# Graph softmax: the maxima of all four heads of a row block in one VectorE instruction, with one signal to ScalarE

## The reference, cut to what matters

```python
msg = xl[src] + xr[dst]
act = jnp.where(msg > 0, msg, NEG_SLOPE * msg)
e = jnp.einsum('ehd,hd->eh', act, att)                  # one score per edge and head
m = jax.ops.segment_max(e, dst, num_segments=n)         # maxima per target node and head
p = jnp.exp(e - m[dst])
denom = jax.ops.segment_sum(p, dst, num_segments=n)
alpha = p / (denom[dst] + 1e-16)
out = jax.ops.segment_sum(alpha[..., None] * xl[src], dst, num_segments=n)
return out.reshape(n, HID) @ W_up
...
x = x + _L1_gnn_ref(...) + _L1_mix_ref(...)             # both added to the residual
```

## Time and profile before

| | |
|---|---|
| time, median of 3 runs | 1725.18 us (1722.89 to 1726.66) |
| the profiled execution's own time | 1725.1 us |
| its span | 1722.8 us |
| TensorE busy | 1674.9 us, 97% |
| VectorE busy | 832.2 us, 48% |
| ScalarE busy | 414.4 us, 24% |
| mean granted TensorE clock | 0.992 |

### The profile page before, as it was taken

One profiled execution on the slowest core, in us unless ns is written; L12 is line 12 of the kernel. 1 busy time (PEld: TensorE's weight loads), 2 busy tenths in 40 slices (PEclk: granted clock), 3 DMA queues, 4 the chain that ended last, 5 costly groups with the idle time before them and its releaser, 6 DMA issues. The chain is left out here.

```text
span 1722.8 us, 21026 instructions
## 1 busy us (share of the span) xinstructions
PE 1674.9 (97%) x7904; PEld 1044.3 (61%) x7904; DVE 832.2 (48%) x1642; ACT 414.4 (24%) x771; POOL 654.2 (38%) x537
## 2 busy tenths in 40 slices
PE   8999999998999999999999999998999999999998
PEld 5466445544444677755477776555766766777633
DVE  5888334562722432154455554767654223222237
ACT  1000000001411001111167773662112222222232
POOL 0566886220000047677787873000031322222213
PEclk9999999999999999999999999999999999999999
DMA  9655114553360044333322221634076999999951
GB/s 346 217 140 158 1 2 126 132 173 82 145 233 5 0 116 115 98 98 101 90 52 55 53 58 43 174 114 161 1 197 200 391 414 407 413 412 412 402 142 60
DMA packets 103755, 281.70 MB, mean 164 GB/s; under 512 B 61745, under 2 KB 69155, under 8 KB 91282
## 3 DMA queue, kind: packets, MB, share of 16 engines
q1 hardware_dynamic: 28755, 218.54, 34.5%
q0 software_dynamic: 67872, 50.79, 13.3%
q10 hardware_dynamic: 7052, 11.35, 2.2%
HBM read 250.37 MB, written 29.80 MB: 163 GB/s over the span
## 5 line engine op out<-in xcount | busy, mean ns | idle before, releaser
L1015 POOL DMA_INDIRECT table_d<-wring x85 | 174.6, 2055 | 111.2 <-issue 68.8
L1409 POOL DMA_INDIRECT wring<-xl_d,wring x85 | 108.5, 1276 | 253.8 <-DMA xr_d<-flat_b 227.9
L1422 POOL DMA_INDIRECT score_d<-wring x85 | 110.9, 1305 | 73.0 <-DMA score_d<-wring 46.4
L469 PE MATMUL bank<-flat_d,wring 128*128 128x312 f32 (+1 forms) x512 | 135.0, 426 | 0.0
L3011 PEld LDWEIGHTS bank<-picked_flat,wring 128*128 128x128 f32 x1152 | 129.4, 192 | 7.7 <-issue 7.7
L3011 PE MATMUL bank<-picked_flat,wring 128*128 128x128 f32 x1152 | 131.3, 276 | 0.0
L1409 POOL DMA_INDIRECT wring<-xr_d,wring x85 | 111.3, 1309 | 25.9 <-issue 23.8
L469 PEld LDWEIGHTS bank<-flat_d,wring 128*128 128x128 f32 x512 | 96.9, 189 | 37.7
L3018 PE MATMUL bank<-wring,picked_flat 128*64 128x256 f32 x640 | 73.3, 382 | 1.2 <-PEq L2485 1.2
L1696 PE MATMUL bank<-wring,flat_d 128*125 128x512 f32 x160 | 71.5, 599 | 0.8 <-ACT flat_c L2224 0.5
L3124 PE MATMUL bank<-wring,region_a 128*125 128x512 f32 x160 | 68.9, 593 | 2.7 <-issue 2.7
(11 more groups left out here) (487 smaller groups left out, 2979.5 us busy)
## 6 DMA issues: line engine op xcount, KB each, us to landing
wring<-in_experts SPq DMA_DIRECT2D x57, 2048.0 KB, 19.5
wring<-in_L_Ws SPq DMA_DIRECT2D x6, 2048.0 KB, 16.6
table_d<-eq_buf SPq DMA_DIRECT2D x2, 3072.0 KB, 27.9
score_d<-no_edge SPq DMA_DIRECT2D x2, 3072.0 KB, 32.8
wring<-table_d POOLq DMA_DIRECT2D x10, 610.4 KB, 7.3
wring<-score_d SPq DMA_DIRECT2D x5, 1093.8 KB
wring<-pid_d ACTq DMA_DIRECT2D x17, 312.5 KB
wring<-in_edge_w ACTq DMA_DIRECT2D x17, 312.5 KB
```

The lines of the kernel that those rows point to most:

```text
L469: ins = pe.matmul(bank[:, 0:n], w[:, k * HALF + m * P:k * HALF + (m + 1) * P], act_t[:, k, at:at + n], start=(k == 0), stop=(k == chunks - 1))
L1015: pool.indirect_dma_start(out=tables_d[b % 2], out_offset=bass.IndirectOffsetOnAxis(ap=edge_at[:, b:b + 1], axis=0), in_=edge_sums[:, b, : ...
L1409: pool.indirect_dma_start(out=to[:, g % 2, j, :], out_offset=None, in_=table, in_offset=bass.IndirectOffsetOnAxis(ap=index[:, b:b + 1], ax ...
L1422: pool.indirect_dma_start(out=score_d, out_offset=bass.IndirectOffsetOnAxis(ap=cell_i[:, b:b + 1], axis=0), in_=logit[:, b, :], in_offset= ...
```

## The change

The four reductions of a block become one instruction with a view that has the head as outer and the node as inner dimension, and writes four maxima. One negation of four values follows, and `tops_made` rises by one for each block instead of two. ScalarE's exponentials wait once for each block, ahead of head 0. What the exponentials signal in turn (`exps_made`, after each pair) stays.

```diff
--- before.py
+++ after.py
@@ -2071,20 +2071,13 @@
                         for _ in edge_logits(v, V_GROUP_AT[n]):
                             pass
 
-                def find_top(t, h):
-
-                    if h == 0:
-                        v.wait_ge(score_in[t % 2], SCORES_FROM[t % 2] + 32 * (t // 2 + 1))
-                    soft.mark(v.tensor_reduce(top[:, t, h:h + 1], scores[:, t % 2, :, h], AX.X, ALU.max))
-                    if h % 2:
-                        after(v, soft)
-                        pair = top[:, t, h - 1:h + 1]
-                        v.tensor_scalar(pair, pair, -1.0, None, ALU.mult).then_inc(tops_made, 1)
-
                 def find_tops(t):
 
-                    for h in range(GH):
-                        find_top(t, h)
+                    v.wait_ge(score_in[t % 2], SCORES_FROM[t % 2] + 32 * (t // 2 + 1))
+                    soft.mark(v.tensor_reduce(top[:, t, :], scores[:, t % 2, :, :].rearrange("r n h -> r h n"), AX.X,
+                                              ALU.max))
+                    after(v, soft)
+                    v.tensor_scalar(top[:, t, :], top[:, t, :], -1.0, None, ALU.mult).then_inc(tops_made, 1)
 
                 late = all_steps(range(LATE_GROUP, GROUPS_E))
                 v.memset(qf[:, :, M:3 * MC], 0.0).then_inc(features_set, 1)
@@ -2264,8 +2257,8 @@
                 def exps(t):
 
                     for h in range(GH):
-                        if h % 2 == 0:
-                            s.wait_ge(tops_made, 2 * t + h // 2 + 1)
+                        if h == 0:
+                            s.wait_ge(tops_made, t + 1)
                         ins = s.activation(probs[:, t % 2, h, :], scores[:, t % 2, :, h], ACT.Exp, bias=top[:, t, h:h + 1])
                         if h % 2:
                             ins.then_inc(exps_made, 1)
```

## The result

The changed kernel took 1733.85 us (median of 9 runs, 1730.80 to 1737.22), the kernel before 1727.80 us beside it. The ratio is 1.0041 with a 95% interval of 1.0027 to 1.0054, or 7.1 us more at 1727.8 (4.7 to 9.3); the two medians lie 6.1 us apart. I had forecast 7.3 us more, and 1732.4 us as the time. In two later comparisons the same pair gave 1.0049 (1.0026 to 1.0071) and 1.0054 (1.0036 to 1.0073). The profiled execution has a span of 1732.3 us against 1722.8, with a mean clock of 0.988 against 0.992.

A forecast was written before the change was run, and what follows sets the result against it. TensorE was taken as the bound, delayed when ScalarE's exponentials start late. A 6.7 us delay plus 0.6 us for the clock gave 7.3 us more, 1732.4 us, with a range of 1727.0 to 1737.0 us.

The forecast's parts named there:

- The price of the reduction: On VectorE, the wide reduction of 2500 strided elements takes 4.70 us, from strided rates of 1.74 to 1.81 ns an element.
- the contiguous rate: On VectorE, elements read in order cost 1.03 ns each, which would make the wide reduction 2.74 us.
- rival 1: Not slower: VectorE's wide reduction takes 2.74 us, TensorE gains nothing, time 1725.0 to 1725.6 us; chance 0.10.
- The estimate of 4.43 us: On VectorE, joining saves three fixed parts of 0.16 us, 0.47 us off the 4.90 of two old pairs.
- The hand-over: ScalarE's exponentials begin 5.01 us after VectorE's first reduction instead of 2.76, so 2.25 us later per block.
- The chain: Late exponentials carry through blocks 0 to 3: ScalarE idles, TensorE waits at fifth banks, 6.7 us in all.
- The clock: TensorE's stops may drop its clock to 0.50, costing 1.5 us; 0.6 us charged for an even chance, part hidden.
- The sum: For the whole kernel, 6.7 us of delay plus 0.6 us of clock, 7.3 us more, giving 1732.4 us.
- rival 2: A middle price: reduction of 3.81 us, exponentials 1.4 us later per block, TensorE held 3.1 us, 1728.2 us; chance 0.10.
- Rival 3: More than forecast: reduction of 5.17 us costs 8.6 us, or 11.6 with low clock after each stop, 1736.7 us; chance 0.13.
- Rival 4: TensorE's rests behind the stage swallow 2 to 5 us of the delay, time 1728 to 1730 us; chance 0.07.
- The stretch behind the stage keeps its length: Behind the softmax stage TensorE is the bound, so its 138 us stay and the delay passes on whole.

The follow-up runs named there:

- e3: Changed kernel with one contiguous maximum of 2500 elements per row shared by all heads, for times only; ratio 0.9996 to the kernel before.
- e1: Changed kernel with the four narrow reductions of before, but one negation and signal after all four; ratio 1.0045 to the kernel before.
- e4: Changed kernel with four unused matmuls put into TensorE's wait ahead of the fifth bank, blocks 0 and 1; ratio 1.0034 to the kernel before.
- e12: Second run of the changed kernel with unused matmuls in TensorE's two waits; ratio 1.0040 to the kernel before.
- e7: Changed kernel, unaltered, run again for a second profile; ratio 1.0049 to the kernel before.
- e11: Changed kernel, unaltered, run again for a third profile; ratio 1.0054 to the kernel before.
- e10: Kernel before with the first negation and signal after three heads, the second after the fourth; ratio 1.0036 to the kernel before.
- e2: Kernel before with two wide reductions of two heads each, each with its own negation and signal; ratio 0.9994 to the kernel before.
- e5: Changed kernel with TensorE's turnings and later steps one product tile later; ratio 1.0016 to the kernel before.
- e8: Kernel before, unaltered, run again for a second profile; ratio 0.9993 to the kernel before.

## Why the prediction was right

**The price of the reduction** was right: 4.70 us forecast, 4692 ns measured as the mean of five. The rate of the strided rows holds for the grouped view, and the contiguous rate, the basis of rival 1, comes only where the elements are read in order (e3). The estimate of 4.43 us, by the Trainium skill's page "VectorE: DVE Perf Modes" (The TRN2 errata), was too low. In its place stands e1: four narrow reductions without a wait between them take 4.79 us, so joining them saves 0.2 us, and not three fixed parts.

**The hand-over** was forecast at 5.01 us and measured at 4.94. **The chain** was right in its places: ScalarE's idle of about 2 us twice and then none, TensorE's waits at the fifth banks of blocks 0 and 1. Without the clock I had 6.7 us, and e4 and e12 with no fall in the stage measure 95.9 - 89.2 = 6.7. The waits in the first profile were 4.55 and 1.94 where I wrote 3.4 and 3.75. The first was longer because the scores came 1.3 us later beside TensorE's tiles (it grows with that distance: 3.30 at 23.37 us in e7, 4.07 at 24.18 in e11, 4.55 at 24.58). The second was shorter because the longer first wait and the low clock behind it had already made TensorE later (by 1.6 us for the clock), as the prediction said it would.

**The clock** was charged with 0.6 us; the three profiles of the changed kernel less e4 and e12 give 96.5 - 95.9 = 0.6. Its parts were an even chance and 1.5 us with some of it hidden; the second fall came in two profiles of three and was worth 1.2 to 1.4 us. With so few profiles the close agreement is partly luck.

**The sum.** The 7.3 us stand beside 7.7 us for the stage in the first profile, 7.2 over three, and 7.1 us in the time. That the last two agree to 0.1 us is luck: the interval of the time reaches from 4.7 to 9.3 us, and in e10 time and stage differ by 3. The 1732.4 us were counted from 1725.18, the median of three runs of before; nine runs gave 1727.80, and the changed kernel took 1733.85.

**The rivals.** Rival 1 needed the contiguous rate, which the wide form does not have. The middle price of rival 2 belongs to a middle hand-over, which e10 made. Rival 3 needed 5.17 us, and for its 11.6 us also 1.5 us for each of two falls, of which the first cost nothing. Rival 4, that 2 to 5 us of the delay are swallowed behind the stage, does not fall by the first comparison alone, whose interval begins at 4.7 us; the third begins at 6.2. Like set beside like, the stretch behind the stage lasts 548.5 us before and 549.2 and 548.4 changed with no fall of the clock at the gate product, and 552.4 and 551.7 with one. "The stretch behind the stage keeps its length" can be said to about 1 us there, while over all kernels it scatters from 548 to 555.

## What to carry to other kernels

A large instruction that joins the work of several small ones also delays the first result to the last. Before joining, look at who waits for the first part: here VectorE saved 0.4 us a block (from the first reduction to the residual add behind it 5.11 us before, 4.73 now), and ScalarE got its first maxima 2.2 us later, in a chain that passes through three blocks before TensorE's deadline. If the join is wanted, join only as far as one signal reaches (e2), or move the reader's deadline first (e5), and count what that costs.

## What the runs showed of the hardware that I had not expected

- Four reductions of 625 floats at a step of four floats, none of which waits for another, take 4.79 us in a row (e1), though the mean of one is 1.29; one of 2500 takes 4.62 to 4.78. In order, 2500 floats take 2.76 (e3).
- The same small stops of TensorE are followed by a low clock in one execution and not in the next, for instance the gate product behind the stage with 5.26, 6.94 and 6.97 us for the same matmuls. In e8 and in before the wait ahead of it is the same 1.57 us. That is 1.7 us for this product alone; with a second fall near 1330, the stretch behind the stage is 3 to 4 us longer.
- A wait of 2.45 us (e10) was followed by the low clock (8.12 us for the product), as were those of 3.30 to 4.55 us and the second waits of 1.78 to 1.99 us (weighted rows of 3.84 to 3.99 us instead of 2.35). One of 1.56 us in e3 at the same place was not (2.35).
